# One block of an adaLN transformer: order of TensorE's products, two roundings on VectorE, experts from rounded parts

## The reference

```
h   = layernorm(x) * (1 + ca) + sa
q,k,v = split(h @ Wqkv + bqkv)          # 16 heads of 8 channels
K   = exp(-(|k|^2 + |q|^2 - 2 k.q) * r_sigma)
x   = x + ga * ((K @ v) @ Wproj + bproj)
h   = layernorm(x) * (1 + cb) + sb
top = the two largest of h @ w_router + b_router over 8 experts
x   = x + gb * sum over the two of (h @ w_expert[e] + b_expert[e])
```

## Time and profile before

| | us |
|---|---|
| median of three runs | 267.37 (266.65 to 267.68) |
| the profiled execution | 267.84 |
| its span, first to last instruction | 266.0 |
| PE busy | 245.1 |
| ACT busy | 171.3 |
| POOL busy | 155.4 |
| DVE busy | 148.0 |

### The profile page before, as it was taken

The page is one execution under the profiler, slowest core; times in us unless marked ns, Lnnn a source line. Parts: engine busy times, 40 slices in busy tenths (PEclk is TensorE's granted clock), DMA queues, the critical chain, the costliest instruction groups (busy, mean ns, idle before and its releaser), DMA issues.

```text
span 266.0 us, 6149 instructions
## 1 busy us (share of the span) xinstructions
PE 245.1 (92%) x2298; PEld 158.7 (60%) x2298; DVE 148.0 (56%) x541; ACT 171.3 (64%) x234; POOL 155.4 (58%) x232
## 2 busy tenths in 40 slices
PE   7879679999999999999999999999999999996860
PEld 6556335666666666666566666666666666564750
DVE  4427104356566665666656566666666555655364
ACT  2445736978777767676767778777768686871010
POOL 3413907583949494949495867677675828072322
PEclk9999956999999999999999999999999999999595
DMA  6232913131323131222313131313131313100000
GB/s 174 77 129 90 326 51 121 42 127 37 118 62 118 62 118 63 108 72 80 101 57 125 42 138 42 135 45 125 56 108 57 114 44 131 49 22 1 20 20 20
DMA packets 20928, 22.80 MB, mean 86 GB/s; under 512 B 1883, under 2 KB 18723, under 8 KB 20899
## 3 DMA queue, kind: packets, MB, share of 16 engines
q1 hardware_dynamic: 20898, 22.41, 25.3%
HBM read 6.65 MB, written 2.12 MB: 33 GB/s over the span
## 4 chain that ended last, share of the span: by engine, by line
PE 84%; DVE 5%; DMA 3%; POOL 3%; issue 2%; ACT 1%; SPq 1%; POOLq 0%; DVEq 0%
PE att_ps L656 23%; PE ffn_ps L744 20%; PE scores L639 10%; PE qkv_ps L665 7%; PE qkv_ps L671 4%; PE mid_ps L714 3%; PE qkv_ps L680 3%; PE mid_ps L700 3%; PE scores L744 2%; PE mid_ps L708 2%; PE qkv_ps L689 2%; PE mid_ps L732 2%; DMA wqkv_sb<-in_L_attn_Wqkv_dram 2%; DVE acc L508 2%; DMA st<-norm_parts 1%
## 5 line engine op out<-in xcount | busy, mean ns | idle before, releaser
L375 ACT ACTIVATE probs<-scores 128x1024 f32<-128x1024 f32 x128 | 124.0, 1021 | 47.3 <-PE scores L639 45.6
L508 DVE SCALAR_TENSOR_TENSOR acc<-ffn_ps,mask,acc 128x128 f32<-128x128 f32 x228 | 64.2, 344 | 58.6 <-PE ffn_ps L744 56.5
L656 PE MATMUL att_ps<-probs,vpad 128*32 128x256 f32 x1024 | 76.0, 392 | 0.0
L744 PE MATMUL ffn_ps<-we_t,h 128*128 128x256 f32 x228 | 61.0, 390 | 0.0
L307 POOL TENSOR_TENSOR ve<-stats,eps 128x2 f32<-128x2 f32 x32 | 6.2, 194 | 73.6 <-DVE stats L495 73.6
L656 PEld LDWEIGHTS att_ps<-probs,vpad 128*32 128x32 f32 x1024 | 30.6, 110 | 18.9 <-issue 1.7
L744 PEld LDWEIGHTS ffn_ps<-we_t,h 128*128 128x128 f32 x228 | 38.9, 190 | 5.0 <-issue 0.8
L639 PE MATMUL scores<-st 32*128 32x256 f32 x512 | 34.3, 335 | 4.3 <-DMA st<-norm_parts 3.6
L639 PEld LDWEIGHTS scores<-st 32*128 32x128 f32 x512 | 20.5, 186 | 26.3 <-issue 19.9
L312 POOL TENSOR_SCALAR x2n<-x_all,stats,rstd 128x128 f32<-128x128 f32 x32 | 25.3, 798 | 1.7
L527 DVE TENSOR_TENSOR qkf<-qkv_ps,bqk_col 128x512 f32<-128x512 f32 x16 | 11.0, 690 | 27.3 <-PE qkv_ps L665 27.3
(11 more groups left out here) (100 smaller groups left out, 272.6 us busy)
## 6 DMA issues: line engine op xcount, KB each, us to landing
st<-hl SPq DMA_DIRECT2D x48, 256.0 KB
rb_all<-rb_rows SPq DMA_DIRECT2D x16, 192.0 KB, 3.3
out_dram<-x_all SPq DMA_DIRECT2D x16, 128.0 KB, 3.1
x_all<-in_L_attn_x_dram SPq DMA_DIRECT2D x1, 1408.0 KB, 8.0
st<-norm_parts SPq DMA_DIRECT2D x32, 32.0 KB
we_sb<-in_L_ffn_w_experts_dram SPq DMA_DIRECT2D x1, 512.0 KB, 5.8
w_mod_sb<-in_L_wmod_dram SPq DMA_DIRECT2D x1, 384.0 KB, 4.2
x_all<-in_L_attn_x_dram SPq DMA_DIRECT2D x1, 384.0 KB, 3.2
```

The lines of the kernel that those rows point to most:

```text
L375: nc.scalar.activation(probs[:, g, 2 * half:2 * half + 2, :], scores[:, 2 * half:2 * half + 2, :], ACT.Exp, scale=two_sigma).then_inc((exp ...
L508: v.scalar_tensor_tensor(acc[:, q, t, :], bank[:, (t * EC + e) * C:(t * EC + e + 1) * C], mask[:, q, t, 0, EC * c + e:EC * c + e + 1].bitc ...
L656: i = pe.matmul(att_ps[r * ROWS:(r + 1) * ROWS, 0:T], heads[:, g * ROWS:(g + 1) * ROWS], probs[:, g, r, t * T:(t + 1) * T], start=(g == 0 ...
L744: i = pe.matmul(f_bank(b, c)[:, t * EC * C:(t + 1) * EC * C], h2[:, b % 2, t * P:(t + 1) * P], we_t[:, c * EC * C:(c + 1) * EC * C], start ...
```

## The change

- PE's step has another order. turn_mask comes right behind pv(k-1, 3), experts(k-3, 3) behind qk_rows, expert_bias right ahead of scores 1, and each pv(k, g) right behind scores g+1. project comes ahead of values, norms behind pv, experts 1 ahead of turn_x2, router behind pv 2.
- project waits for acc_init in place of m_sb. turn_x2 loses its wait for acc_init and expert_bias its wait for x1_ok.
- experts(b, c) makes three float32r products for each of its two token halves: high part of h2 by high part of the weights, low by high, high by low. The parts of the weights are made once on DVE in step 0, those of h2 in every step on DVE (h2_hi by a copy, h2_lo by a subtraction), behind the experts' chunk 1 and ahead of the logits.
- The high parts of q and k are copied by DVE right behind qkf, no longer by ACT.
- The second normalisation's x2n is written by DVE behind the experts' chunk 0. POOL still computes rstd, and it writes xn of block k+2 only behind rstd of block k-1. In step k from 0 on, its squares and low parts so come ahead of xn.
- DVE does the x_all addition and the statistics ahead of vpad.
- ACT copies the mask between the two exp operations of group 0 and the bias into acc ahead of group 1.

```diff
@@ PE
-                    pe.wait_ge(m_sb, b)
+                    pe.wait_ge(acc_init, b)
...
             def experts(b, c):
-                if b == 0 and c == 0:
-                    pe.wait_ge(wet_sb, 1)
+                if c == 0:
+                    pe.wait_ge(h2_parts, b + 1)
+                    if b == 0:
+                        pe.wait_ge(we_ok, 1)
...
                 for t in range(NT):
-                    i = pe.matmul(f_bank(b, c)[:, t * EC * C:(t + 1) * EC * C], h2[:, b % 2, t * P:(t + 1) * P],
-                                  we_t[:, c * EC * C:(c + 1) * EC * C], start=True, stop=True)
+                    dst = f_bank(b, c)[:, t * EC * C:(t + 1) * EC * C]
+                    hi, lo = h2_hi[:, b % 2, t * P:(t + 1) * P], h2_lo[:, b % 2, t * P:(t + 1) * P]
+                    es = slice(c * EC * C, (c + 1) * EC * C)
+                    pe.matmul(dst, hi, we_hi[:, es], start=True, stop=False)
+                    pe.matmul(dst, lo, we_hi[:, es], start=False, stop=False)
+                    i = pe.matmul(dst, hi, we_lo[:, es], start=False, stop=True)
                 i.then_inc(f_ps, 1)
 
             def step(k):
                 if has(k):
                     qk_scores(k, 0)
                 if has(k - 1):
                     pv(k - 1, 3)
+                if has(k - 2):
+                    turn_mask(k - 2)
                 if has(k + 1):
                     qk_rows(k + 1)
-                if has(k - 2):
-                    turn_mask(k - 2)
                 if has(k - 3) and k <= NB:
                     experts(k - 3, 3)
+                if has(k - 2):
+                    expert_bias(k - 2)
                 if has(k):
                     qk_scores(k, 1)
+                    pv(k, 0)
+                if has(k - 1):
+                    project(k - 1)
                 if has(k + 1):
                     values(k + 1)
-                if has(k - 1):
-                    project(k - 1)
-                if has(k):
-                    pv(k, 0)
                 if has(k - 2) and k <= NB:
-                    expert_bias(k - 2)
                     experts(k - 2, 0)
                 if has(k):
                     qk_scores(k, 2)
+                    pv(k, 1)
                 if has(k + 1):
                     norms(k + 1)
-                if has(k):
-                    pv(k, 1)
-                if has(k - 1):
-                    turn_x2(k - 1)
                 if has(k - 2) and k <= NB:
                     experts(k - 2, 1)
+                if has(k - 1):
+                    turn_x2(k - 1)
                 if has(k):
                     qk_scores(k, 3)
+                    pv(k, 2)
                 if has(k - 1):
                     router(k - 1)
-                if has(k):
-                    pv(k, 2)
@@ DVE
+            def normalise(b, par):
+                dve.wait_ge(rstd2, b + 1)
+                for t in range(NT):
+                    i = v.tensor_scalar(x2n[:, par, t * C:(t + 1) * C], x_all[:, b, t * C:(t + 1) * C],
+                                        stats[:, 1, par, 3 * t + 1:3 * t + 2], rstd[:, 1, t:t + 1], ALU.subtract, ALU.mult)
+                i.then_inc(x2n_ok, 1)
...
+                    dve.wait_ge(qkf_ok, k + 2)
+                    v.tensor_copy(hl[:, 0:4:2, :], qkf[:, :, :]).then_inc(hi_ok, 1)
...
                 if has(k - 2):
                     experts(k - 2, 0)
+                if has(k - 1):
+                    normalise(k - 1, odd)
...
+                if k == 0:
+                    dve.wait_ge(wet_sb, 1)
+                    v.tensor_copy(we_hi[:, :], we_t[:, :]).then_inc(we_hi_ok, 1)
+                    dve.wait_ge(we_hi_ok, 1)
+                    v.tensor_tensor(we_lo[:, :], we_t[:, :], we_hi[:, :].bitcast(F32), ALU.subtract).then_inc(we_ok, 1)
...
+                if has(k - 1):
+                    dve.wait_ge(h2_ok, k)
+                    v.tensor_copy(h2_hi[:, odd, :], h2[:, :]).then_inc(h2_hi_ok, 1)
+                    dve.wait_ge(h2_hi_ok, k)
+                    v.tensor_tensor(h2_lo[:, odd, :], h2[:, :], h2_hi[:, odd, :].bitcast(F32), ALU.subtract).then_inc(h2_parts, 1)
@@ POOL
                 if has(k + 2):
-                    normalise(0, xn[:, par, :], k + 2, par, bn1, ve1, rstd1, xn_ok)
+                    rsqrt(0, k + 2, par, bn1, ve1, rstd1)
+                    if k < 0:
+                        normalise(k + 2, par)
...
                 if has(k - 1):
-                    normalise(1, x2n[:, odd, :], k - 1, odd, bn2, ve2, rstd2, x2n_ok)
+                    rsqrt(1, k - 1, odd, bn2, ve2, rstd2)
+                if has(k + 2) and k >= 0:
+                    normalise(k + 2, par)
```

More of the change, by code:

```diff
@@ L109, in adaln_block @@
         x2n = sb("x2n", [P, 2, NT * C])
-        h2 = sb("h2", [P, 2, T])
+        h2 = sb("h2", [P, T])
+        h2_hi = sb("h2_hi", [P, 2, T], F32R)
+        h2_lo = sb("h2_lo", [P, 2, T], F32R)
         logit = sb("logit", [P, NT, NE])
@@ L206, in adaln_block @@
         h2_ok = sem("h2_ok")
+        h2_hi_ok = sem("h2_hi_ok")
+        h2_parts = sem("h2_parts")
+        we_hi_ok = sem("we_hi_ok")
+        we_ok = sem("we_ok")
         r_ps = sem("r_ps")
@@ L309, in normalise @@
                 nc.gpsimd.tensor_tensor(rstd[:, n, :], ve[:, n, :], expo[:, :], ALU.pow).then_inc(rstd_ok, 1)
-                pool.wait_ge(rstd_ok, b + 1)
+            def normalise(b, par):
+                pool.wait_ge(rstd1, b + 1)
                 for t in range(NT):
-                    i = nc.gpsimd.tensor_scalar(dst[:, t * C:(t + 1) * C], x_all[:, b, t * C:(t + 1) * C],
-                                                stats[:, n, par, 3 * t + 1:3 * t + 2], rstd[:, n, t:t + 1], ALU.subtract, ALU.mult)
-                i.then_inc(done, 1)
+                    i = nc.gpsimd.tensor_scalar(xn[:, par, t * C:(t + 1) * C], x_all[:, b, t * C:(t + 1) * C],
+                                                stats[:, 0, par, 3 * t + 1:3 * t + 2], rstd[:, 0, t:t + 1], ALU.subtract, ALU.mult)
+                i.then_inc(xn_ok, 1)
             def step(k):
@@ L384, in step @@
                     exp(k, 0, 0)
+                if has(k - 2):
+                    act.wait_ge(m_ps, k - 1)
+                    nc.scalar.copy(mask_t[:, :], m_bank(k - 2)[0:2 * NE, 0:T]).then_inc(m_sb, 1)
+                if has(k):
                     exp(k, 0, 1)
@@ L398, in step @@
                     nc.scalar.copy(be_hi[:, :], be_sb[:, :]).then_inc(be_hi_ok, 1)
+                if has(k - 2):
+                    act.wait_ge(b_ps, k - 1)
+                    if k > 3:
+                        act.wait_ge(gated_ok, k - 3)
+                    nc.scalar.copy(acc[:, par, :, :].rearrange("p t c -> p (t c)"), m_bank(k - 2)[:, 0:NT * C]).then_inc(acc_init, 1)
                 if has(k):
@@ L411, in step @@
                     act.wait_ge(x2t_ps, k)
-                    nc.scalar.activation(h2[:, odd, :], mid_ps[:, 0:T], ACT.Identity, bias=shift_col[:, 1, k - 1:k],
+                    nc.scalar.activation(h2[:, :], mid_ps[:, 0:T], ACT.Identity, bias=shift_col[:, 1, k - 1:k],
                                          scale=scale_col[:, 1, k - 1:k]).then_inc(h2_ok, 1)
@@ L546, in step @@
                     ln_stats(1, b, odd, bn2)
+                if has(k + 1):
+                    dve.wait_ge(v_ps, k + 2)
+                    v.tensor_tensor(vpad[:, odd, :, :, 0:HD],
+                                    qkv_ps[:, 0:NT * C].rearrange("p (t h d) -> p t h d", t=NT, d=HD),
+                                    bq_all[:, 2 * C:3 * C].rearrange("p (h d) -> p h d", d=HD).unsqueeze(1).broadcast_to([P, NT, H, HD]),
+                                    ALU.add).then_inc(v_ok, 1)
                 if has(k - 2):
                     experts(k - 2, 0)
+                if has(k - 1):
+                    normalise(k - 1, odd)
                 if has(k + 1):
```

38 lines of the change are left out of this document (10 added, 28 removed).

## The result

Four runs of the changed kernel on one chip took 255.86 us (median; 255.46 to 256.95), four of the kernel before beside them 267.01 (265.31 to 267.68). The ratio is 0.9598, with a 95% interval of 0.9543 to 0.9653. The forecast was 254.0, its range 250.5 to 262. So direction and size came out, 1.9 us short of the forecast. The profiled execution took 256.95, with a span of 255.2 against 266.0 before.

A forecast was written before the change was run, and what follows sets the result against it. PE's own order was taken to bound the step, 13.78 to 12.75: eleven steps 11.3, step 2 0.5, step 14 0.9, step 15 1.2, tail costing 0.5, together 13.4 off 267.84: 254.4, or 254.0 on the median's footing; range 250.5 to 262.

The forecast's parts named there:

- A change of shape costs 0.20: On PE, each change of tile shape between groups of products costs 0.20 us; 15 changes per step become 12.
- The order, 0.6 less 0.15: PE's step: three fewer shape changes save 0.6 us, less 0.15 for turn_mask's uncovered load and bias's two added loads.
- rival (4): Bias and scores share no shape: one change more, 0.2 a step, 256.5 us; chance 0.55 together with the forecast.
- A float32r product costs 0.11: PE's experts: a float32r product of 256 columns takes about 0.11 us, saving 0.20 per group, 0.8 a step.
- Rival (3): float32r at full shape runs at the float32 instruction's rate: step 15.0, about 283 us; chance 0.04.
- The sheet: PE's work per step added up without any wait: 13.78 - 0.8 - 0.6 + 0.15 = 12.55 us.
- DVE's additions, about 1.6: DVE's added work per step: high copy 0.42, h2_hi 0.28, h2_lo 0.43, x2n halves 0.45, about 1.6 us in all.
- The transfer behind norm_parts, 3.39: DMA from norm_parts' start to next scores takes 3.39 us; with norm_parts at 9.2 the next step may start at 12.6.
- rival (1): x2n's second half on DVE waits for POOL at the shared port: step 13.2, 258.8 us; chance 0.27.
- Rival (2): DVE loses the port at both x2n halves, behind xn then gated: step 14.0, about 270 us; chance 0.08 with other DVE-order cases.
- Step 14, forecast -0.9: Step 14, counted apart from the eleven full steps, was to get 0.9 us shorter.
- Step 15 and the tail: Step 15 saves 1.2 us (three changes, four groups); the tail costs 0.5, last experts waiting for h2_parts, turn_mask behind them.

The follow-up runs named there:

- e2: Changed kernel with float32 experts again, high copies on ACT and x2n on POOL, so only the new order is left: 259.66 us, ratio 0.9801.
- e4: Changed kernel with values ahead of pv 0 and project behind it, one shape change more per step: 257.88 us, ratio 0.9713.
- e3: Changed kernel with the experts alone undone: float32 products, no parts of h2 or weights; order and moves to DVE stay: 260.68 us, ratio 0.987.
- e5: Changed kernel with one product (high by high) instead of three in experts' chunks 1 and 2: 247.64 us, ratio 0.929.
- e10: Changed kernel where POOL in steps 14 to 16 starts gated only after DVE has written x2n: 254.34 us, no ratio.
- e6: Changed kernel with POOL's gated and x_all addition ahead of xn instead of behind it: 258.35 us, ratio 0.9672.
- e9: Changed kernel with another end: last h2 parts and mask ahead of block 14's chunks 2 and 3, mask turned before block 15's experts: 248.08 us, ratio 0.9332.
- e8: Changed kernel with the high copies of q and k back on ACT: 257.67 us, ratio 0.9567.

## Why the prediction was right, and where it was off

**PE bounds the step: right.** In e2 to e4 the step followed PE's order, and in the changed kernel PE is busy for 12.67 of 12.67 us.

**A change of shape costs 0.20: right,** by e4. **The order, 0.6 less 0.15:** measured 0.49 (e2, e3) against 0.45; how it splits into the two was not measured. Bias and scores do share a shape, as their loads lie among each other in the changed kernel with no pause between, and rival (4) is out:

```profile
114.84 0.18 PEld L761 LDWEIGHTS mid_ps<-be_parts,mask_t 16*128 16x128 f32 x1
114.85 0.19 PEld L671 LDWEIGHTS scores<-st 32*128 32x128 f32 x3
114.94 0.18 PEld L761 LDWEIGHTS mid_ps<-be_parts,mask_t 16*128 16x128 f32 x1
114.95 0.40 PEld L671 LDWEIGHTS scores<-st 32*128 32x128 f32 x5
```

**A float32r product costs 0.11: nearly.** It is 0.115, and a group takes 0.90 in place of 1.06, so four save 0.64 where I had 0.8. Rival (3) is out. The 0.645 between e3 and the changed kernel agrees with that, so nothing hit PE's order in the step. I had 12.55 plus 0.2 for waits (the sum as written gives 12.53). The sheet was 0.1 too short and the 0.2 was not there: two small errors of opposite sign, the 0.2 the larger, so the step came out 0.1 below the forecast.

**DVE's additions, about 1.6:** the high copy 0.427 (0.42), h2_hi 0.28 (0.28), h2_lo 0.43 to 0.57 (0.43), the x2n pair 0.61 (0.45). A tensor_scalar with two scalars per row costs 0.335 for 128x128, more than the cast of 0.215 that I took for it. It didn't matter: norm_parts starts 9.15 behind the step's first scores, as my places said (9.2).

**The transfer behind norm_parts, 3.39: too long.** The bound is 3.2 (e5), so the step has 0.3 of slack at its place where I had almost none.

**The shared port, rival (1): right mechanism, wrong neighbour.** xn does not hold x2n (0.61 beside it, 0.59 in e10's step 14 with POOL idle). gated and the addition behind it do, 1.33 to 1.36, but in the steady step x2n is over before gated starts. Provoked in e6, it makes the pair longer by 0.7 and the step by 0.13. Rival (2) would have needed xn to hold it too. The Trainium skill, "SBUF — State Buffer", section "Who interferes with whom", makes the lock hold for any operation of GpSimd beside DVE's two-port modes. e6 agrees; the row at 119.44 beside xn doesn't show it, and the measurement decides.

**Step 14, forecast -0.9, measured -0.11.** This term failed. I read it as a step like the others with one thing less. Two things differ in it. POOL has no xn, so gated meets x2n and norm_parts starts 0.43 later (9.58 behind the step's start in place of 9.15); and from there to the scores it took 3.92 in place of 3.2. 9.58 and 3.2 would have been 12.78, which e5 bears out with 12.81, so 0.72 is the transfer's and nearly all that the term missed by.

**Step 15 and the tail, forecast -1.2 and +0.5, measured +3.41.** This is the larger miss, 4.1 us. The first half stood: with the order alone (e2) the stretch is 36.7, 1.5 below before's 38.2. With the moves to DVE (e3) it is 38.2 again, x2n there taking 1.55 and 1.53, and with the products 41.6. The granted clock differs between these (0.91, 0.87, 0.80 on the mean, 0.82 before), so the differences are not the work's alone. The 0.5 was mis-sized. The sentence named the mechanism (the last experts wait for h2_parts, and turn_mask stands behind them) and priced only the wait. It left out that PE then has 24 products to do in front of the mask, at the lower clock for 5.1 us, with DVE's last additions behind them. e9, which takes that out, gives back 7.1 us, its higher clock included; e10 by itself gives 2.0 at the same clock, the port's share in steps 15 and 16 (x2n 1.55 and 1.54 there, 0.6 in e10).

Steps 2 to 13 gave 1.5 more than forecast and the start 0.8; step 14 and what follows took 4.9 more. The total came within 1% because these offset each other in part, and that is luck: the start's 0.8 belongs to no term of the forecast. The 0.4% that I took for the scatter of this kernel was also too small: in the rounds behind the experiments the kernel before ran from 262.0 to 268.7.

## What to carry to other kernels

A steady step read from PE's own loads (price of a shape change, price of a product) can be forecast to 1%. But a kernel with such a step has a first and a last one in which neighbours are missing: write the places of those out too, since an operation that is free beside one neighbour is held by the next (x2n beside xn, x2n beside gated), and an order that is right in the loop puts finished work behind unfinished at the end. Here two edits at the end took 10 us off it, the clock's share included, nearly as much as the whole change (11.2).

## What the hardware showed beyond that

- DVE's tensor_scalar pair takes 0.61 beside POOL's tensor_scalar and 0.59 beside nothing, but 1.18 to 1.55 beside POOL's tensor_tensor. The other way round, POOL's sq went from 1.04 to 1.28 when DVE's high copy came to overlap it, and is at 1.04 again in e8. One line of the changed kernel over all blocks (ns, minimum, median, maximum):

```profile
L335 POOL TENSOR_TENSOR sq<-qkf x15: 1040/1280/1282, 24.2 to 203.6; 128x512 f32<-128x512 f32 x15
```

- A float32 product with its own weights of 128 columns takes two instructions of 0.216, a float32r one 0.115: three float32r products cost 0.345 against 0.43, so the split pays 20% of PE's time for them, and only where the rounding of the parts is hidden.
- Packets of 16 KB that carry instructions take 0.9 to 1.8 us each, 19 of them in the changed kernel. In step 14 a transfer of 64 KB in two DMAs that crossed one was late by 0.4 to 2.0 us; in other steps most that crossed one were not.
